# Graph attention: gathers by slot, or gathers by tile and a copy from tile to slot

## The reference

```python
h = relu(layernorm(x));  x = x + rgcn(rgcn(h))          # two RGCN layers
h = relu(layernorm(x));  x = x + elu(bn(gat(elu(bn(gat(h))))))   # two GAT layers

# RGCN: W[r] = sum_b w_comp[r,b] * basis[b]
agg = segment_sum(h[src], dst * 16 + rel);  out = relu(sum_r agg[:, r] @ W[r] + h @ loop_w + bias)

# GAT, 4 heads of 32, edges plus one self loop for each node
xw = x @ W;  e = leaky_relu(al_s[src] + al_d[dst], 0.2)
ee = exp(e - segment_max(e, dst)[dst])
out = segment_sum(ee * xw[src], dst) / segment_sum(ee, dst)[dst] + b
```

## Time and profile before

| | |
|---|---|
| median of 3 runs | 4563.35 us (4553.26 to 4567.41) |
| span of the profiled execution | 4547.9 us |
| the median above that span | 15.45 us |
| POOL busy | 3132.4 us, 69% |
| PE busy | 3121.2 us, 69% |
| DVE busy | 2544.8 us, 56% |
| ACT busy | 1107.5 us, 24% |
| gathers of the GAT passes (L2098) | 1660, busy 1603.1 us |
| gathers of the RGCN passes (L2081) | 1564, busy 1497.3 us |

### The profile page before, as it was taken

How to read it: one execution, slowest core, us unless ns; L and a number is a source line. 1 busy time by engine, 2 the same in 40 slices (tenths; PEclk the granted TensorE clock), 3 DMA queues, 4 the chain that set the end, 5 groups by cost and what they waited for, 6 DMA issues and landing times.

```text
span 4547.9 us, 63220 instructions
## 1 busy us (share of the span) xinstructions
PE 3121.2 (69%) x13439; PEld 2273.6 (50%) x13439; DVE 2544.8 (56%) x9924; ACT 1107.5 (24%) x2623; POOL 3132.4 (69%) x3271
## 2 busy tenths in 40 slices
PE   7976777777756666666646676767674666676766
PEld 3444444444434444444435555656563555565655
DVE  6534444444434455555556566767674667676776
ACT  3311222222200111111122233323332223332333
POOL 1057777777767777777677777777727777777772
PEclk9966889888855555555555566656665556665666
DMA  6633444444432222222222222222212222222222
GB/s 232 259 111 98 151 148 154 149 150 154 154 97 62 65 65 65 66 66 66 61 54 54 54 54 54 54 54 54 54 39 58 55 55 55 55 54 54 54 55 73
DMA packets 168049, 394.03 MB, mean 87 GB/s; under 512 B 57414, under 2 KB 92036, under 8 KB 150532
## 3 DMA queue, kind: packets, MB, share of 16 engines
q0 software_dynamic: 103616, 215.16, 17.9%
q10 hardware_dynamic: 37536, 102.42, 6.0%
q1 hardware_dynamic: 26532, 72.39, 4.3%
HBM read 229.57 MB, written 160.17 MB: 86 GB/s over the span
## 4 chain that ended last, share of the span: by engine, by line
PE 39%; DMA 15%; DVE 14%; issue 13%; POOL 11%; ACT 4%; DVEq 2%; SPq 1%; ACTq 0%; POOLq 0%
DMA Gr<-Ttab,GID 12%; PE B L1837 11%; PE B L1979 8%; POOL Gr L2098 8%; PE B L1737 6%; PE B L1799 3%; POOL Gr L2081 3%; DMA Gr<-Gtab,SRC 3%; DVE XA L1128 2%; DVE XA L935 2%; DVE Sr L1027 2%; PE B L1911 1%; PE B L1895 1%; ACT hold L1534 1%; DVE Gr L1103 1%
## 5 line engine op out<-in xcount | busy, mean ns | idle before, releaser
L2098 POOL DMA_INDIRECT Gr<-Gtab,SRC x1660 | 1603.1, 966 | 584.2 <-issue 448.5
L2081 POOL DMA_INDIRECT Gr<-Ttab,GID x1564 | 1497.3, 957 | 604.6 <-PE B L1837 272.8
L1837 PE MATMUL B<-Gr,Sr 128*128 x3328 | 999.0, 410 | 596.5 <-SPq L2114 328.6
L1837 PEld LDWEIGHTS B<-Gr,Sr 128*128 128x128 f32 x3328 | 731.3, 270 | 1051.9 <-issue 1036.4
L1979 PE MATMUL B<-Gr,Sr 128*128 128x136 f32 x3328 | 959.3, 432 | 132.9 <-DVE XA L1128 80.9
L1979 PEld LDWEIGHTS B<-Gr,Sr 128*128 128x128 f32 x3328 | 740.3, 295 | 203.7 <-DVE XA L1128 130.3
L935 DVE TENSOR_TENSOR XA<-XA,B 128x128 f32 x1664 | 471.6, 283 | 571.8 <-PE B L1837 521.3
L1128 DVE TENSOR_TENSOR XA<-XA,B 128x136 f32 x1664 | 480.8, 289 | 294.2 <-PE B L1979 237.9
L924 DVE TENSOR_SCALAR Sr<-iota,DL 128x128 f32<-128x128 f32 x1664 | 493.3, 300 | 20.6 <-issue 16.2
L1737 PE MATMUL B<-XA,H 128*128 128x512 f32 x664 | 412.5, 709 | 1.7 <-DVE H L602 0.4
L1027 DVE TENSOR_SCALAR Sr<-iota,DL 128x128 f32<-128x128 f32 x1664 | 370.2, 295 | 0.0
(11 more groups left out here) (287 smaller groups left out, 3001.2 us busy)
## 6 DMA issues: line engine op xcount, KB each, us to landing
Ttab<-Sr ACTq DMA_DIRECT2D x83, 1024.0 KB, 4.2
Ttab<-Sr SPq DMA_DIRECT2D x51, 1024.0 KB, 3.9
Gr<-Gtab,SRC POOLq DMA_INDIRECT x1660
Gr<-Ttab,GID POOLq DMA_INDIRECT x1564
Gtab<-Gr ACTq DMA_DIRECT2D x83, 66.0 KB
X1D<-Gr ACTq DMA_DIRECT2D x83, 64.0 KB
out<-Sr SPq DMA_DIRECT2D x12, 256.0 KB
Gtab<-XA SPq DMA_DIRECT2D x5, 528.0 KB, 3.8
```

What stands on the lines that cost most here:

```text
L1837: e.matmul(B[banks[s % len(banks)]][:, 0:P], selr(s), Gr[:, bass.ds(o, P)], start=True, stop=True).then_inc(slot_mm, 1)
L2081: e.indirect_dma_start(out=Gr[:, (sn + 1) % TG * P:((sn + 1) % TG + 1) * P], out_offset=None, in_=Tt[L][:, :], in_offset=bass.IndirectOffs ...
L2098: e.indirect_dma_start(out=Gr[:, (s % GR) * CW:(s % GR) * CW + 132], out_offset=None, in_=T2[L][0:NPAD][:, :], in_offset=bass.IndirectOffs ...
```

## The change

In the GAT passes GpSimd gathers by tile too: 782 gathers a pass, into a ring of 64 tiles (`TILES`, 132 floats each) of its own. GpSimd also reports them: before each fourth gather it waits for the four tiles before the last three, and raises a count by 4 (`landed[2 + L]`). A gather may start when the copy of the slot 16 before its own number has landed.

SyncE, whose queue had next to nothing to do in these passes, copies each slot's rows from its tile to its slot (`to_slots`): 830 transfers a pass inside the on-chip memory, 128 rows of 528 bytes, each with the tile's place taken from a register. Before each it waits for the tile's count (against a register), for the copy 16 before it, and, from slot 64 on, for the product of the slot 64 before it. Every 16 slots it loads two times 16 registers. The slot ring shrinks from 96 to 64 slots. ScalarE's `als` waits for the copies of the chunk instead of the gathers.

`SRC` now holds the row numbers by tile, made by one shift of `GID` on VectorE; the products, copies and list parts that made it by slot (28 products, 2 copies, 3 VectorE operations) are gone. VectorE makes `TIX` in 16-bit form and scales `OFT` from 128 to 132 floats before the GAT passes. To make room, several small buffers move into others (`dx`, `penF`, `penL`, `ads` into `DST`, `CONT`, `PBK` and `PFK` into one tensor at partitions 0, 32 and 64, the flat lists' parts from `hold` to `Gr`).

```diff
-GR = 96
+GR = 64
+TW = 132
+TQ = 4
+NTQ = 8
-        Gr = sb("Gr", [P, GR * CW])
+        Gr = sb("Gr", [P, GR * CW + TG * TW])
-        SRC = sb("SRC", [P, NS], i32)
+        SRC = sb("SRC", [P, NT], i32)
+        def wait_tiles(e, L, g):
+            e.wait_ge(tiles[L][g % NTQ], 16 * TQ * (g // NTQ) + 16 * min(TQ, NG - TQ * g))
+        def wait_spread(e, n):
+            e.wait_ge(spread[n % NSG], 16 * (n // NSG + 1))
...
+            e.wait_ge(ta.sem, ta.at("gid1"))
+            then(e.tensor_scalar(out=SRC[:, :], in0=GID[:, 0:NT], scalar1=4, scalar2=None, op0=ALU.arith_shift_right), "src")
...
+            e.tensor_scalar(out=OFT, in0=OFT, scalar1=TW / P, scalar2=None, op0=ALU.mult).then_inc(late, 1)
...
-                        wait_gather(e, 2 * NG + L * NGS + 3 * k)
+                        wait_spread(e, L * NGS + 3 * k)
...
-                for n in range(n0 + NSG, min(n0 + 2 * NSG, 2 * NG + (L + 1) * NGS)):
-                    wait_gather(e, n)
+                for n in range(end - NSG, end):
+                    wait_spread(e, n)
                 then(e.copy(v3(dc[:, 1, :]), G3(c, 128, 132).rearrange("p s h -> p h s")), "als")
...
-            yield from select("src", [f3(spb[2]), f3(spb[3])], (ta, "oft1"), (tv, "tl1"))
-            yield from select("il", [f3(lb)], (ta, "src1"), (tv, "lb"))
+            yield from select("il", [f3(lb)], (ta, "oft1"), (tv, "lb"))
...
-                for s in range(NGS):
-                    n = 2 * NG + L * NGS + s
-                    wait_gather(e, n - NSG)
-                    if s >= GR:
-                        e.wait_ge(gat_mm, L * NS + s - GR + 1)
+                for t in range(NG):
+                    g = t // TQ
+                    if t % TQ == TQ - 1 and g:
+                        wait_tiles(e, L, g - 1)
+                        e.sem_inc(landed[2 + L], TQ)
+                    back = t - TG + NGS - NG
+                    if back >= 0:
+                        wait_spread(e, L * NGS + back)
                     e.indirect_dma_start(
-                        out=Gr[:, (s % GR) * CW:(s % GR) * CW + 132], out_offset=None, in_=T2[L][0:NPAD][:, :],
-                        in_offset=bass.IndirectOffsetOnAxis(ap=SRC[:, s:s + 1], axis=0)).then_inc(gat[n % NSG], 16)
+                        out=TILES[:, (t + 1) % TG * TW:((t + 1) % TG + 1) * TW], out_offset=None, in_=T2[L][0:NPAD][:, :],
+                        in_offset=bass.IndirectOffsetOnAxis(ap=SRC[:, t:t + 1], axis=0)).then_inc(tiles[L][g % NTQ], 16)
+                for g in range((NG + 1) // TQ - 1, -(-NG // TQ)):
+                    wait_tiles(e, L, g)
+                    e.sem_inc(landed[2 + L], TQ)
...
+        def to_slots(e, L, kregs, oregs):
+            for s in range(NGS):
+                n = L * NGS + s
+                if s % 16 == 0:
+                    e.reg_load(kregs, TIX[:, s:s + 16])
+                    e.reg_load(oregs, OFT[0:1, s:s + 16])
+                if n >= NSG:
+                    wait_spread(e, n - NSG)
+                if s >= GR:
+                    e.wait_ge(gat_mm, L * NS + s - GR + 1)
+                e.wait_ge(landed[2 + L], kregs[s % 16])
+                o = off(e, oregs[s % 16], (TG - 1) * TW)
+                e.dma_start(Gr[:, s % GR * CW:s % GR * CW + TW], TILES[:, bass.ds(o, TW)]).then_inc(spread[n % NSG], 16)
...
             rest(e, rest2_store, "r2s")
+            e.wait_ge(rest_done, 2)
+            e.wait_ge(late, 6)
+            to_slots(e, 0, kregs, oregs)
             for w0, w1 in STORED:
...
+            e.wait_ge(pr_mm, NPAIR)
+            to_slots(e, 1, kregs, oregs)
```

More of the change, by code:

```diff
@@ L45 @@
 XC = 16
+NST = 33
 SG = 8
@@ L154, in build @@
         H = sb("H", [P, 4, P])
-        lw = [sb(f"lw{l}", [P, P]) for l in range(2)]
+        lwp = [sb(f"lw{l}", [P, P + (1 if l == 0 else 0)]) for l in range(2)]
+        lw, pen = [x[:, 0:P] for x in lwp], lwp[0][:, 0:129]
         rb = [sb(f"rb{l}", [P, P]) for l in range(2)]
@@ L209, in build @@
         built_v = sem("selection_made")
-        landed = [sem(f"landed{l}") for l in range(2)]
+        landed = [sem(f"landed{l}") for l in range(4)]
+        tiles = [[sem(f"tiles{l}_{i}") for i in range(NTQ)] for l in range(2)]
+        spread = [sem(f"spread{i}") for i in range(NSG)]
         slot_mm, slot_add = sem("slot_products"), sem("slot_added")
@@ L261, in build @@
         Pm = Gr[0:RF, 10000:10000 + TPR * NS // 2].bitcast(bf16).rearrange("p (b s) -> p b s", b=TPR)
[L262 to L269, removed]
+        EB = 10000 + TPR * NS // 2
+        spb = [Gr[0:RF, EB + k * (RL // 2):EB + (k + 1) * (RL // 2)].bitcast(bf16) for k in range(3)]
+        EI = EB + 3 * RL // 2
+        spi = Gr[0:RF, EI:EI + RL].bitcast(i32)
+        wbi = Gr[0:RF, EI + RL:EI + RL + 7].bitcast(i32)
+        wbf = Gr[0:RF, EI + RL + 7:EI + RL + 14]
+        wb2 = Gr[0:RF, EI + RL + 14:EI + RL + 28].bitcast(bf16)
+        slb = Gr[0:RF, EI + RL + 28:EI + RL + 32].bitcast(bf16)
+        sli = Gr[0:RF, EI + RL + 32:EI + RL + 39].bitcast(i32)
+        slh = Gr[0:RF, EI + RL + 39:EI + RL + 46].bitcast(i32)
         slk = small[:, 0:4].bitcast(bf16)
@@ L656, in tables_vector @@
                 yield
[L657 to L666, removed]
+            then(e.tensor_scalar(out=spi, in0=fdi, scalar1=7, scalar2=7, op0=ALU.arith_shift_right, op1=ALU.arith_shift_left), "ti0")
+            yield
+            after("ti0")
+            then(e.tensor_copy(spb[0], spi), "th0")
+            after("th0")
+            then(e.tensor_tensor(spb[1], dF, spb[0], ALU.subtract), "tl0")
+            yield
+            yield
+            yield
             then(e.tensor_copy(lb, lF), "lb")
@@ L701, in tables_vector @@
                                      op1=ALU.arith_shift_left), f"ofs{h}")
+                then(e.tensor_scalar(out=TIX[:, hsl[h]], in0=TIL[32:33, hsl[h]], scalar1=1.0, scalar2=None, op0=ALU.max), f"tix{h}")
                 if h == 0:
@@ L1321, in tables_scalar @@
             yield "early"
-            half("src", SRC, 0)
-            yield
-            half("src", SRC, 1)
-            yield
             e.wait_ge(tg.sem, tg.at("of31"))
@@ L2116, in relay @@
                 e.sem_inc(landed[L], 1)
+        def to_slots(e, L, kregs, oregs):
[11 more added lines that the diff above has]
+                e.dma_start(Gr[:, s % GR * CW:s % GR * CW + TW], TILES[:, bass.ds(o, TW)]).then_inc(spread[n % NSG], 16)
         def sync(e):
+            kregs, oregs = registers(e, "tile", 16), registers(e, "place", 16)
             def flat_load(t, name, o, sem_):
```

57 lines of the change are left out of this document (28 added, 29 removed).

## The result

The changed kernel takes **4603.46 us** (median of 4 runs, 4600.93 to 4606.18), the kernel before 4563.07 us (4 runs, 4553.26 to 4567.41): ratio 1.009, 95% interval 1.0077 to 1.0104. The forecast was 4450 us, range 4436 to 4530. Time and sign were both wrong.

A forecast was written before the change was run, and what follows sets the result against it. GpSimd's gather pace was taken to bound the GAT passes. Span 4547.9 - 122.0 (fewer gathers) + 8 (pass ends) + 1 (chunks) = 4434.9 us, plus 15.45 outside the span: 4450 us, range 4436 to 4530.

The forecast's parts named there:

- Moved buffers cost nothing: the same operations on the same shapes: Buffers moved to make room: no added time, 0 us.
- nothing, at most 1 us each: New VectorE operations (`src`, `tix`, `OFT` scaling), in gather-paced passes or beside a GAT pass's first gathers: no cost, at most 1 us each.
- GAT gathers, -122.0 us: Both GAT passes: 48 fewer gathers each, at 1.2766 and 1.2644 us, save 61.3 and 60.7 us, counted in full.
- the landing eats a part: Rival, GAT passes: GpSimd's group waits hold for landings; half of 390 holding 0.3 us gives +58, 4508 us; chance 0.18.
- SyncE, 0.7 us a slot: SyncE's copy loop in the GAT passes: 0.7 us a slot, holding nothing up to 1.20 us.
- End of a pass, +4 us each: After each GAT pass's last gather: two copies issued (1.4 us) and the last landing (2.5 us), +8 us in all.
- The signs named in the prediction: Expected profile: gather gaps 0.30 us, SyncE idle at times, `als` waiting 6 to 10 us for copies in plain chunks.
- Chunks without slack, +1 us: GAT chunks that close windows fall up to 2 us behind, the next plain chunk makes it up: +1 us in all.
- What lies outside the span, 15.45 us: Whole kernel: the median lies 15.45 us above the profiled span, added to the forecast span of 4434.9 us.
- The three rivals: Landing eats a part (4508 us, 0.18), SyncE becomes the bound (4789 us, 0.10), no change (4563 us, 0.04).
- the 10% for slower: Rival, `to_slots`: SyncE sets the pace, slower from 1.264 us a slot; at 1.40 us, 4789 us; chance 0.10.

The follow-up runs named there:

- b16: The kernel before with only its tile numbers (`TIX`) made 16-bit, at partition 64 in place of 32: 4708.85 us, ratio 1.0348 to the kernel before.
- t32: The changed kernel with 32-bit tile numbers again and a maximum with 1 ahead of each wait: 4451.17 us (ratio 0.9774) on A, 5584.27 us (1.0159) on B.
- A: Not a run: the two chips on which the kernel before takes 4553 us.
- B: Not a run: the three chips on which the kernel before takes 5500 to 5560 us.

## Why the prediction was wrong

**The step that failed** is "Moved buffers cost nothing: the same operations on the same shapes", with "nothing, at most 1 us each" for `tix`. The write of the 16-bit table was priced, the reading of it was put at nothing, though the table was no longer the same: `TIX` had become 16-bit. `TIX` is read by TensorE's queue in the two RGCN passes, 104 times, and the load's row stood in front of me, as 1.1 us, and was used for SyncE alone. The right question was who reads each buffer whose type changes. Missed: **+155.3 us**, shown by b16 (+155.6) and, taken away, by t32 (-145.6 in that pass); the last 9.7 go with the longer load of the neighbouring table.

**The pass was read as having slack.** The earlier trace rows has PE busy for 646.56 of 860 us in the first RGCN pass, which looks like 25% of room. There is next to none: in the window of the same bounds the changed kernel has

```profile
400.00:1260.00 860.00, 576.64 (x1991) 353.84 (x1989) 311.31 (x1372) 182.29 (x344) 597.87 (x624) 0.80 0.40 132
```

that is, PE's matmuls and GpSimd's gathers fall by 11% and 7% together. What the busy share leaves went to the queue's loads and to short waits for VectorE (113.6 us before), which takes turns with TensorE. The gathers' gaps of 0.30 us in that pass told that GpSimd was at its own pace, and hid that TensorE only just kept up: at 700 us 348 gathers had begun and about 353 products, the last of which reads a tile begun four or five gathers earlier.

**GAT gathers, -122.0 us:** -115.4 measured (-59.8 and -55.6). The count was right and the pace 1.278 and 1.271 us in place of 1.277 and 1.264. The line's own instructions and idle time, against the earlier trace rows:

```profile
L2115 POOL DMA_INDIRECT Gr<-Gtab,SRC x1564: 942/955/1791, 2432.9 to 4515.9; - x196
its engine sat idle before it (us, times) until:
  issue: 463.1, 1517
  DMA Gtab<-XA: 66.1, 1
  DVEq L989: 13.9, 1
  DMA Gr<-Gtab,SRC: 8.2, 27
```

27 gaps are put down to the group waits, 8.2 us in all, but that is 0.30 us each, the usual gap: the waits held nothing, as forecast. The 6.6 us that are missing lie mostly in the gathers themselves, on average 969 ns in place of 966 (5 us in 1564). The rival "the landing eats a part" got nothing of its 58 us from the waits, though the DMA share rose to 0.44, over the 0.37 that I took for it (windows, after):

```profile
2430.00:3440.00 1010.00, 687.43 (x3861) 578.66 (x3861) 687.73 (x2557) 325.99 (x789) 761.12 (x782) 0.61 0.44 109
```

The Trainium skill (DMA: Bandwidth & Descriptors, Issuing engines are not separate DMA queues) says that another issuer saves only issue time; by this trace that is what was saved. In the chain that ended last the landings of these gathers took 2.4 to 3.7 us at that share, against 2.5 to 3.4 before.

**SyncE, 0.7 us a slot:** about 1.0, in three parts. The issue of an on-chip copy took 0.507 us, the row that I took it from 0.338; a 16-bit load 3.77 in place of 1.1, which is 0.17 a slot; and the rest, waits and register work, 0.2. It stayed under the 1.20 at which it would bind, so the term cost nothing on A. But the room was an eighth (SyncE waits for 269 of 1991 us; a fifth in t32) and not 40%, and on B GpSimd waited for copies.

**End of a pass, +4 us each:** +5.2 and +4.7. ScalarE's last `als` waits for the copies (timeline of ACT, after, against the earlier trace rows):

```profile
3439.93 0.42 ACT L1558 COPY hold<-Gr 128x128 f32<-128x128 f32 x1 [3.15 <-DMA Gr<-Gr]
...
4524.02 0.42 ACT L1558 COPY hold<-Gr 128x128 f32<-128x128 f32 x1 [2.58 <-DMA Gr<-Gr]
```

The last copy's issue begins at 4522.1, so it takes 1.9 us from issue to use, where I took 2.5. The estimate of 2.2 us by the Trainium skill's figures (same page, Anatomy of one DMA, which are for the GpSimd path) is nearer. The term was larger because of what came before it: with the 3.37 us of the earlier trace rows for the last landing, 2.9 us pass between the landing and that issue, about three copies at 1.0 us, where I took two at 0.7. The signs named in the prediction were right in part only: 12 of the 52 `als` copies no longer wait at all (40 waits, 249 us; before 52 waits, 389 us), so in those chunks something else than the copies came last. The gathers went on meanwhile, and on A it cost nothing that the table shows.

**Chunks without slack, +1 us**, is not to be told apart from the rest. **What lies outside the span, 15.45 us:** 1.8 us in the run that was profiled, and 1.7 to 2.0 in every run for which both are known. The 15.45 mixed it with the scatter between executions: a span of 4547.9 belongs to a time of about 4550 us, below all four runs of before. The sum in span was 4434.9, the span of t32, the change as I had priced it, is 4452.4.

**The sign.** The sum missed the span by 169.5 us: 155.3 in the first RGCN pass, 7.4 in the GAT passes, 6.8 in the small rest. The three rivals were all put inside the GAT passes; the 10% for slower stood on SyncE and came true by another mechanism.

t32 is the version that beats both kernels where before takes 4553 us, by 2.3%; where it takes 5500 us, the kernel before stays ahead of all that were tried.

## What to carry to other kernels

When a change alters a buffer's type or place, list every reader of it, the queues' register loads among them, and price the read in each pass where it stands. A busy share below 100% is no slack: in the pass with slack TensorE waited for tiles 297 times, in the one without 73 times, most of these where its own loads stood. A wait's name doesn't settle it either, since a load ahead of a wait is counted under it; putting a known load on the queue and measuring does. And when work is handed to an engine that "has nothing to do", price its loop from its own operation, and keep the room wide; what had an eighth to a fifth to spare on one chip was late on another.

## What the runs showed of the hardware

- A load of 16 registers from on-chip memory took 1.104 us from a 32-bit table (1.28 in t32 and its like) and 3.97 us from a 16-bit one, on TensorE's queue; 3.77 us on SyncE's. One register took 0.302 us and four 0.333.
- The issue of a copy from on-chip memory to on-chip memory, 128 rows, took 0.507 us at 528 bytes a row and 0.509 at 264.
- The same program took 4553 us on two chips and 5500 to 5560 on three others, with gathers of the same length (957 to 966 ns on average) and 443 and 497 us more of gaps ahead of them; what makes the gaps is open.
